# A recurrence on one core: the addends of both scans moved into PSUM, the seeds of the update gate behind the scans

## What is computed

```
def step(h, xs):
    xzt, xrt, xht = xs
    z = sigmoid(xzt + h @ U_z + vz)
    r = sigmoid(xrt + h @ U_r + vr)
    hh = tanh(xht + r * h @ U + vh)
    h_new = (1.0 - z) * h + z * hh
    return (h_new, h_new)
...
x = x + L0(x, cond);  x = x + scan(step) over xz = x @ W_z, xr = x @ W_r, xh = x @ W
```

## Time and profile before

| | |
|---|---|
| median of 3 runs | 5869.0 us (5865.66 to 5869.28) |
| the profiled execution | 5866.45 us, its span 5864.7 us |
| busy share | PE 98%, PEld 96%, DVE 91%, ACT 71%, POOL 0% |
| chain that ended last | PE 88%, DVE 9%, issue 2% |
| granted TensorE clock | 0.996 of full speed |
| DMA | 23 GB/s mean, 6.4% of the queues' span |

### The profile page before, as it was taken

How to read it: one execution, slowest core, us unless ns; L and a number is a source line. 1 busy time by engine, 2 the same in 40 slices (tenths; PEclk the granted TensorE clock), 3 DMA queues, 4 the chain that set the end, 5 groups by cost and what they waited for, 6 DMA issues and landing times.

```text
span 5864.7 us, 509556 instructions
## 1 busy us (share of the span) xinstructions
PE 5728.9 (98%) x200328; PEld 5628.1 (96%) x200328; DVE 5322.7 (91%) x47287; ACT 4185.8 (71%) x29549; POOL 8.3 (0%) x32
## 2 busy tenths in 40 slices
PE   8999999999999999999999999999999999999999
PEld 8999999999999999999999999999999999999999
DVE  6999999999999999999999999999999999999998
ACT  3777777777777777777777777777777777777776
POOL 0000000000000000000000000000000000000000
PEclk8999999999999999999999999999999999999999
DMA  3000000000000000000000000000000000000000
GB/s 93 22 20 20 22 20 22 22 18 22 20 22 20 22 18 22 21 22 20 20 22 20 22 22 18 22 20 22 20 22 18 22 21 22 20 20 22 20 22 20
DMA packets 80764, 133.66 MB, mean 23 GB/s; under 512 B 12336, under 2 KB 18480, under 8 KB 80304
## 3 DMA queue, kind: packets, MB, share of 16 engines
q1 hardware_dynamic: 80304, 129.81, 6.4%
HBM read 20.46 MB, written 8.65 MB: 5 GB/s over the span
## 4 chain that ended last, share of the span: by engine, by line
PE 88%; DVE 9%; issue 2%; ACT 0%; DVEq 0%; POOL 0%; POOLq 0%
PE quad L298 53%; PE pair_z L298 26%; PE ps_p L261 9%; DVE quad L577 3%; DVE h_part L621 2%; DVE z_fac L613 1%; DVE z_fac L607 1%; DVE rh_part L595 0%; ACT r_term L411 0%; DVE pair_z L577 0%; PE pair_z L249 0%; DVE h_fac L644 0%; DVE h_safe L647 0%; DVE oT L651 0%; DVE y_next L543 0%
## 5 line engine op out<-in xcount | busy, mean ns | idle before, releaser
L298 PE MATMUL quad<-h_part,u_part 128*128 128x48 f16 (+1 forms) x65568 | 2048.0, 183 | 108.4 <-DVE h_part L621 103.1
L298 PEld LDWEIGHTS quad<-h_part,u_part 128*128 128x128 f16 x65568 | 1854.0, 96 | 204.0 <-DVE h_part L621 151.6
L298 PE MATMUL quad<-rh_part,u_part 128*128 128x48 f16 (+1 forms) x65536 | 1998.5, 182 | 0.1
L298 PE MATMUL pair_z<-h_part,u_part 128*128 128x48 f16 (+1 forms) x65552 | 1940.2, 182 | 0.0
L577 DVE TENSOR_REDUCE quad<-quad 128x2 f32<-128x4 f32 (+1 forms) x12290 | 1881.1, 167 | 62.5 <-PE quad L298 9.4
L298 PEld LDWEIGHTS quad<-rh_part,u_part 128*128 128x128 f16 x65536 | 1847.8, 96 | 2.7 <-ACT quad L394 0.2
L298 PEld LDWEIGHTS pair_z<-h_part,u_part 128*128 128x128 f16 x65552 | 1785.1, 96 | 0.0
L621 DVE TENSOR_TENSOR_SCAN h_part<-z_fac,n_term 128x20 f16<-128x20 f32 x8192 | 1509.5, 196 | 8.3 <-issue 8.3
L419 ACT ACTIVATE n_term<-quad 128x4 f32<-128x4 f32 x8192 | 1359.7, 173 | 103.1
L411 ACT ACTIVATE r_term<-quad 128x8 f32<-128x8 f32 x4098 | 580.1, 184 | 1191.4 <-DVE quad L577 1191.4
L394 ACT ACTIVATE quad<-xp 128x8 f32 (+2 forms) x6146 | 1040.5, 183 | 30.9 <-issue 28.5
(11 more groups left out here) (80 smaller groups left out, 1942.3 us busy)
## 6 DMA issues: line engine op xcount, KB each, us to landing
w_stage<-w_in SPq DMA_DIRECT2D x384, 256.0 KB, 2.3
x_tok<-in_x SPq DMA_DIRECT2D x68, 128.0 KB, 2.6
out_dram<-o_tok SPq DMA_DIRECT2D x66, 128.0 KB, 2.3
mlp_w<-in_L_cond_W SPq DMA_DIRECT2D x2, 1024.0 KB, 6.9
u_raw<-in_L_cond_U_r SPq DMA_DIRECT2D x1, 1024.0 KB, 5.9
u_raw<-in_L_cond_U_z SPq DMA_DIRECT2D x1, 1024.0 KB, 7.9
u_raw<-in_L_cond_U SPq DMA_DIRECT2D x1, 1024.0 KB, 10.7
w_in<-in_L_cond_W_r SPq DMA_DIRECT2D x4, 256.0 KB, 10.0
```

What stands on the lines that cost most here:

```text
L298: return nc.tensor.matmul(to, u_part[:, g, part, k, m * P:(m + 1) * P], parts[:, at:at + run].unsqueeze(1).broadcast_to([P, repeats, run]) ...
```

## The change

Nothing of the matmuls changes. Four things do.
1. `r_term` and `n_term` are no longer in SBUF but in unused columns of PSUM: `r_term` in banks 2 and 3, `n_term` by chunks in banks 2, 4, 5, 3 (`NT`). All six banks are now one tensor, `six`. Their constants are set once at the start by DVE.
2. The copy of the old state is four ACT instructions of 8 elements, `old_state(q)`: chunks 0 and 3 at the head of the step, ahead of the sigmoids of r, behind a new wait for `h_ok`; chunk 1 behind the sigmoid of z0, chunk 2 behind that of z1.
3. `zn` is two DVE instructions of 4 elements (`moved`): chunks 1 and 2 between the scans of chunks 2 and 3, chunks 0 and 3 behind the last scan.
4. The seed of z for the next step moves from between tanh 1 and 2 to behind the last tanh, and now waits for `hs3`, the end of the last scan; PE's update gate waits for it (`z_seeds`). The seed behind it waits for `keep_ok`. The copy to `hist` moves to between tanh 2 and 3. `store_projection` moves from the head of a body's last step to the end of the step before, ahead of the seed of z.

```diff
-        h_cur, z_now, z_inv, cand = h_fac[:, :, 1], z_fac[:, :, 3], z_fac[:, :, 7], n_term[:, :, 0]
+        h_cur, z_now, z_inv = h_fac[:, :, 1], z_fac[:, :, 3], z_fac[:, :, 7]
...
-        quad = ctx.enter_context(nc.psum_tensor("quad", [P, K, 512], F32))
-        pair_z = ctx.enter_context(nc.psum_tensor("pair_z", [P, 2, 512], F32))
+        six = ctx.enter_context(nc.psum_tensor("six", [P, K + 2, 512], F32))
+        quad, pair_z = six[:, 0:K, :], six[:, K:K + 2, :]
...
+        RT_AT, NT_AT = 256, 448
+        OUTER, INNER = (2, slice(0, K, K - 1)), (4, slice(1, K - 1, 1))
+        NT = [2, 4, 5, 3]
+        def n_term(first, count=2):
+            return six[:, first:first + count, NT_AT:NT_AT + B * H_STEP].rearrange("p q (b c) -> p q b c", c=H_STEP)
+        r_term = [quad[:, 2 + hf, RT_AT:RT_AT + HS * RH_STEP].rearrange("p (s c) -> p s c", c=RH_STEP) for hf in range(2)]
...
-            def update_gate(hf):
+            def update_gate(hf, t1):
+                if hf == 0:
+                    pe.wait_ge(s["z_seeds"], t1)
                 tiles(Z, range(hf * HC, (hf + 1) * HC), range(K), closes=True).then_inc(s[f"z{hf}_mm"], 1)
...
-                A(n_term[:, quarter[q], 0:8:7], twice(quad[:, AT[q], H_SUM:H_SUM + B]), ACT.Tanh, scale=scale_reg[H]).then_inc(s[f"n{q}_in"], 1)
-            def old_state():
-                return A(n_term.rearrange("p s (a c) -> p s a c", a=2)[:, :, :, 1:4:2],
-                         h_cur.unsqueeze(2).unsqueeze(3).broadcast_to([P, S, 2, 2]), ACT.Copy)
+                A(n_term(NT[q], 1)[:, 0, :, 0:8:7], twice(quad[:, AT[q], H_SUM:H_SUM + B]), ACT.Tanh, scale=scale_reg[H]).then_inc(s[f"n{q}_in"], 1)
+            def old_state(q):
+                return A(n_term(NT[q], 1)[:, 0].rearrange("p b (a c) -> p b a c", a=2)[:, :, :, 1:4:2],
+                         h_cur[:, quarter[q]].unsqueeze(2).unsqueeze(3).broadcast_to([P, B, 2, 2]), ACT.Copy)
...
-                    if proj is not None and u == K:
-                        act.wait_ge(s["proj_mm"], act.snap(proj[2] + 2))
-                        store_projection(proj[0], proj[1], 0)
-                        store_projection(proj[0], proj[1], 1).then_inc(s["xp_ok"], 1)
...
+                    act.wait_ge(s["h_ok"], act.snap(t0 + (u + 1)))
+                    old_state(0)
+                    old_state(K - 1)
                     for hf in range(2):
                         reset_gate(hf, t1)
...
-                    old_state()
+                    old_state(1)
                     update_gate(1, t1)
+                    old_state(2)
+                    for q in range(K - 1):
+                        candidate(q, t1)
                     A(hist[:, :, bass.ds(prv, 1)], h_cur.unsqueeze(2), ACT.Copy)
-                    candidate(0, t1)
-                    candidate(1, t1)
-                    seed(pair_z, Z, slice(0, K, 1), nxt)
-                    candidate(2, t1)
-                    candidate(3, t1)
+                    candidate(K - 1, t1)
+                    if proj is not None and u == K - 1:
+                        act.wait_ge(s["proj_mm"], act.snap(proj[2] + 2))
+                        store_projection(proj[0], proj[1], 0)
+                        store_projection(proj[0], proj[1], 1).then_inc(s["xp_ok"], 1)
+                    act.wait_ge(s["hs3"], act.snap(t0 + (u + 2)))
+                    seed(pair_z, Z, slice(0, K, 1), nxt).then_inc(s["z_seeds"], 1)
...
+                    act.wait_ge(s["keep_ok"], t1)
                     seed(quad[:, 2:4], H, slice(0, K, K - 1), nxt)
...
-                    V.tensor_tensor_scan(h_part[:, q * RUN:q * RUN + B * H_STEP], row(z_fac, quarter[q]), row(n_term, quarter[q]),
+                    V.tensor_tensor_scan(h_part[:, q * RUN:q * RUN + B * H_STEP], row(z_fac, quarter[q]), n_term(NT[q], 1).rearrange("p q b c -> p (q b c)"),
                                          0.0, ALU.mult, ALU.subtract).then_inc(s[f"hs{q}"], 1)
+                def moved(banks):
+                    first, chunks = banks
+                    kb3 = lambda a: a[:, :].rearrange("p (k b) -> p k b", b=B)[:, chunks]
+                    return V.tensor_tensor(kb3(zn), kb3(z_raw), n_term(first)[:, :, :, 0], ALU.mult)
...
                 new(2)
+                moved(INNER)
                 new(3)
-                V.tensor_tensor(zn[:, :], z_raw[:, :], cand, ALU.mult).then_inc(s["keep_ok"], 1)
+                moved(OUTER).then_inc(s["keep_ok"], 1)
```

45 lines of the change are left out of this document (28 added, 17 removed).

## The result

| | before | after |
|---|---|---|
| median | 5868.41 us (5865.66 to 5869.28, 4 runs) | 6201.77 us (6201.33 to 6202.13, 4 runs) |
| span of the profiled execution | 5864.7 us | 6199.9 us |
| granted TensorE clock | 0.996 | 0.996 |

The ratio is 1.0568, with a 95% interval of 1.0552 to 1.0585: 333 us slower. The forecast was 6150 us in a range of 6010 to 6270.

What follows compares the result with a forecast made beforehand. The prediction took a ring over PE, DVE and ACT to bound the kernel. 5866.5 + 154 (late seed) + 134 (stores ahead of it) = 6154.5, rounded down to 6150 us, 4.8% slower, range 6010 to 6270.

Steps and rivals of the forecast that it cites:

- a ring over PE, DVE and ACT: Whole step: a ring over three engines, not PE's products, sets the step's 2.78 us.
- The seed of z: Update gate's first load: PE 0.09 us late, 0.07 net, plus 0.005 for PSUM; 154 us over 2048 steps.
- the 0.02 of the forecast: Candidate's products: their 0.02 us wait per step for the second r*h scan vanishes in the update gate's lateness.
- the piece of `zn`: DVE's hole before the fourth scan: piece starts at 3001.89, fourth scan at 3001.96 to 3001.97 instead of 3001.95.
- My 0.005 for PSUM on the path: DVE scans reading addends from PSUM: 0.005 us longer on the path per step, bounds nothing and 0.02 per scan.
- The stores: Stores ahead of the seed of z: PE 0.36 us later still, taken as 0.35, 134 us over 384 steps.
- Queued behind the seed: ACT: other seed (0.13), two small copies (0.12 each), first sigmoid of r at 2.79 against 2.77, covered by update gate's lateness.
- Turning steps: Turn blocks: in some of 128 steps DVE is late itself and swallows the delay; sum rounded down to 6150 us.
- Stores' register work hidden: Rival: the stores' register work runs while ACT waits for scans, second term nothing, 6020 us; chance 0.10.
- The wait adds no register time: Rival: waiting for `hs3` adds no register time, seed starts at 3002.20 and is hidden, 6015 us; chance 0.08.
- DVE is held longer by PSUM: Rival: scans and the `zn` piece at PSUM's upper bound, 0.10 us a step, 205 us on top, 6355; chance 0.08.
- Faster: Rival: seed and stores both hidden, the earlier sigmoid's gain remains, 5846 us; chance 0.05.

Runs made afterwards that it cites:

- r_term alone: Kernel before with only the addends of r*h (r_term) moved to PSUM, timed twice: 5843.34 us (0.9956) and 5842.06 us (0.9953).
- the loop by two: ACT's inner loop written out for two bodies: 6224.26 us (1.0602) on the changed kernel, 5986.49 us (1.0197) on the kernel before.
- the return in the hole: Changed kernel with ACT's loop ending behind the last tanh, both seeds at its head, second seed waiting for h_ok: 6111.61 us (1.0412).
- the constants alone: Kernel before plus only DVE's eight writes of constants into PSUM at the start, r_term still in SBUF: 5866.53 us (1.0002).

## Why the prediction came out as it did

The time was in the range and the sign right, but in part by luck: a cost that the forecast left out was met for more than half by others that it had too large. Step by step:

**What bounds the kernel** held: a ring over PE, DVE and ACT, in which what is put ahead of a seed or sigmoid appears in the step's length.

**The seed of z, 0.075 us in all 2048 steps, 154 us: too large.** In the second to fourth steps it was 0.042, 0.033 and 0.058. The seed's own arithmetic is right: in the median of the 384 third steps of a body its end-to-start distance from the fourth scan is 0.129 (forecast 0.13), and from the scan's end to the first load of the update gate it is 0.367 (forecast 0.37). Wrong was the rest. That second distance was not 0.28 before but 0.30 (I had read it in one step), and the fourth scan does not end 0.02 later but, counted from the first load of the reset gate, 0.022 sooner (0.530 before, 0.508 after). So the update gate is 0.046 late and not 0.09. Of that the rest of the ring gave 0.035 back in these steps (from the update gate's first load to the end of the step it is 1.919 in the median, where it was 1.954), 0.025 of it within the candidate's 32 loads, 0.779 instead of 0.804: that is the 0.02 of the forecast. The median third step is only 0.009 longer, the mean 0.033. These are differences to the kernel before, and hold the gains of the shorter instructions as well; against the kernel whose seed waits for the inner `zn` the late seed costs 0.089, 0.040 and nothing in the second to fourth steps, in one of them more than the 0.075 forecast. I had put the piece of `zn` at a start of 3001.89 and the fourth scan behind it; that part is right in shape (the piece at 3002.49, the scan at 3002.58, 0.09 apart). But scans and tanh became shorter. From PSUM the state's scans took, in the groups by line and shape of the changed kernel:

```profile
L651 DVE TENSOR_TENSOR_SCAN h_part<-z_fac,six 128x20 f16<-128x20 f32 x8192 | 1459.9, 190 | 14.2 <-issue 14.2
...
L432 ACT ACTIVATE six<-six 128x4 f32<-128x4 f32 x8192 | 1276.6, 158 | 182.4 <-DVE six L607 75.8
L436 ACT ACTIVATE six<-h_fac 128x8 f32<-128x8 f32 x8192 | 1262.3, 171 | 117.9 <-issue 117.9
```

and from SBUF, in those of the kernel before:

```profile
L621 DVE TENSOR_TENSOR_SCAN h_part<-z_fac,n_term 128x20 f16<-128x20 f32 x8192 | 1509.5, 196 | 8.3 <-issue 8.3
L419 ACT ACTIVATE n_term<-quad 128x4 f32<-128x4 f32 x8192 | 1359.7, 173 | 103.1
```

196 against 190 ns for the scan, 173 against 158 for the tanh. My 0.005 for PSUM on the path had the wrong sign: the runs with r_term alone give 0.02 us a step back. I took a plain addition (159 against 148 ns in the earlier trace rows) for the nearest row, and the scan did not behave like it.

**The stores, 0.35 us on top, in 384 steps: right.** 0.075 + 0.35 = 0.425 was forecast for the fifth step, 0.411 came. Without the stores it lost 0.368, in all 139 us; forecast 134. The issue ahead of the stores is 113.1 us in 384 times, 0.29 each, as in the earlier trace rows.

**"Queued behind the seed": this step failed.** I listed the other seed, two copies and the first sigmoid as all that stands behind the seed, and priced them at 0.12 each. Between the fifth step of a body and the first of the next there stands also the return of ACT's inner loop: a branch and the body's register instructions, 0.42 us in the chain above. I had looked at register instructions only where they belong to a line that the diff touches. The return had always been there. It lay in the hole in which ACT waits for the sums of r, and the change filled that hole with the two copies and pushed the seeds into it. 0.307 us in 384 steps, 118 us; the loop by two shows it in the one kernel and its absence in the other, the return in the hole gives 0.216 of it back by another way. The rest of the first step's 0.367, 0.060, is about what the ordinary steps lost. I had named the hole itself ("the stores filled a hole in which ACT waits for r's sums anyway") and not asked what else lay in it.

**Turning steps:** -13 us, which I had only rounded for. The first turning step alone gives -19, and the constants alone give -19 there too.

In one table, us:

```
                                      forecast    measured
body steps 1 to 4, seed late            115          74
fifth step, seed and stores             163         158
return of ACT's inner loop                0         118
turning steps                            10         -13
sum                                     288         337
```

288 is 0.075 x 2048 + 0.35 x 384; of the 118 that I missed, 41, 5 and 23 were met by what I had too large elsewhere. The number was nearer than the reasoning.

**The rivals.** *Stores' register work hidden*: no, 0.29 of issue stayed. *The wait adds no register time*: no, 0.129 from the scan's end to the seed, where the condition was 0.03. *DVE is held longer by PSUM*: no; had the estimate from the Trainium skill (Perfetto Trace Analysis, Optimizing Scalar/DVE Operations) of 0.065 us more for each access held, the scans would take some 0.26 and 0.28 where they take 0.190 and 0.207. The measurement decides, and the figure of the Trainium skill does not describe these scans. Another rule of the Trainium skill, that ACT writes faster into PSUM (ScalarE: Activation LUTs, Step-by-step: what each stage is for), agrees with this trace: tanh 158 against 173 ns, sigmoid 153 in the mean against 184. *Faster*: not with all four edits, but the first alone for r is.

**What stays open.** Whether fetched instructions are the whole reason that the longer loop costs ACT up to 3.8 us; and why eight instructions more on DVE move single steps by 0.15 to 0.6 us. The queue for instructions moved 450 packets with and without them, and that these steps stand at fixed places of a block speaks for the place of DVE's loops in its program, but no run shows it. Of the gain of r_term in PSUM, 0.02 a step, what belongs to the shorter scan (5 ns each) and what to the earlier sigmoid (19 ns) was not taken apart.

## What to carry to other kernels

When work moves on an in-order engine, write down everything that stood in the hole it moves into, with the loop's branch and register instructions between the last instruction of a body and the first of the next: what is hidden there costs nothing until the hole is filled, and then it is on the path in full. Compare step lengths by their place in the loop and not by their mean; here two places of the loop held 299 of 337 us, and each named its own cause. Repairs that count on the same hole don't add up, and one of them may undo the other; an empty copy of an edit (the same instructions, no use made of them) shows what its mere presence costs. When a change makes PE idle for microseconds, read the granted clock too: part of what a step seems to cost may be the clock's.

## What the runs showed of the hardware

- The return of a loop on ACT, exposed, took 0.42 us in the chain (3000.01 to 3000.43) and 0.307 us of the step. Hidden it took nothing (2818 against 2820 ns).
- The same loop written with two bodies made ACT idle up to 3.8 us once a block, 112.9 us in 31 times, in the kernel before, and up to 2.8 us in the changed one. The queue for instructions moved 606 packets instead of 450, three of them in each of these 31 stretches (one in the changed kernel).
- Behind 2.27 us without a product TensorE's granted clock was 1.2 instead of 2.4 GHz; the second turning steps took 3.78 to 3.98 us in 31 blocks where the one at the full clock took 2.83.
- A DVE scan whose addends lie in PSUM is shorter than one from SBUF: 190 against 196 ns for 20 elements, 207 against 212 for 28.
- A weight load is recorded for 0.095 us and the next one starts 0.025 later, so the list of waits misses lateness below 0.07: it has 353 waits for the seed, the starts 1939 late steps.
- Eight instructions more at DVE's start took 0.59 us from one step in 64 and added 0.15 to 0.36 to single steps at fixed places (the medians of the 45th, 50th and 55th step of a block: 2959, 3092 and 3141 ns against 2786), in sum nothing: 1.0002.
